# A row maximum carried from chunk to chunk in the score stage of a three-layer attention kernel

## The reference, cut to what matters

```
attn = einsum('bhnd,bhmd->bhnm', qr, kr) + mask          # N = 2304 positions
out  = einsum('bhnm,bhmd->bhnd', softmax(attn, axis=-1), vr)
lepe = conv_general_dilated(v, dw_w, 5x5, feature_group_count=C) + dw_b
```

## Time and profile before

| | |
|---|---|
| median of 3 runs | 3760.14 us (3759.69 to 3761.54) |
| the profiled execution, its own time | 3757.02 us |
| its span from first to last instruction | 3754.9 us |
| mean granted clock of TensorE over the span | 0.963 |
| busy, share of the span | PE 92%, PEld 71%, DVE 74%, ACT 55%, POOL 42% |

### The profile page before, as it was taken

How to read it: one execution, slowest core, us unless ns; L and a number is a source line. 1 busy time by engine, 2 the same in 40 slices (tenths; PEclk the granted TensorE clock), 3 DMA queues, 4 the chain that set the end, 5 groups by cost and what they waited for, 6 DMA issues and landing times. The chain is left out here.

```text
span 3754.9 us, 97899 instructions
## 1 busy us (share of the span) xinstructions
PE 3470.2 (92%) x30782; PEld 2676.2 (71%) x30782; DVE 2794.1 (74%) x6801; ACT 2050.7 (55%) x3661; POOL 1594.4 (42%) x671
## 2 busy tenths in 40 slices
PE   7749999999999999999999999999499999999676
PEld 4437777777777777777777777777287777788555
DVE  6858888888888888888888888886465655544598
ACT  3236666666666666666666666665145454544433
POOL 2336565656656566565656656565100000000223
PEclk8879999999999999999999999999699999999788
DMA  5434224224224223223422422221420201000001
GB/s 172 139 97 125 91 90 129 91 83 111 90 91 128 90 91 105 89 90 100 118 90 97 107 80 97 91 88 46 148 81 14 81 14 40 1 1 0 29 13 38
DMA packets 122409, 307.36 MB, mean 82 GB/s; under 512 B 15609, under 2 KB 85292, under 8 KB 101548
## 3 DMA queue, kind: packets, MB, share of 16 engines
q1 hardware_dynamic: 122284, 305.78, 26.5%
HBM read 251.43 MB, written 54.31 MB: 81 GB/s over the span
## 5 line engine op out<-in xcount | busy, mean ns | idle before, releaser
L729 DVE CUSTOM_DVE_ANT_0 c_S<-c_Sps,mask_tiles 128x768 f32<-128x768 f32 x1728 | 1618.6, 956 | 432.2 <-PE c_Sps L780 391.5
L670 ACT ACTIVATE c_PT<-c_Tps 128x512 f32<-128x512 f32 x2592 | 1428.5, 605 | 872.0 <-PE c_Tps L791 809.4
L642 POOL TENSOR_SCALAR c_S<-c_S,c_row_max 128x2304 f32<-128x2304 f32 x576 | 1411.0, 2450 | 966.4 <-DVE c_row_max L740 966.4
L791 PE MATMUL c_Tps<-ident,c_S 128*128 128x128 f32 x10368 | 1398.6, 273 | 4.1 <-ACT c_PT L670 4.1
L791 PEld LDWEIGHTS c_Tps<-ident,c_S 128*128 128x128 f32 x10368 | 1225.5, 140 | 150.6 <-ACT c_PT L670 9.7
L780 PE MATMUL c_Sps<-c_K,c_Q 96*128 (+1 forms) x3456 | 853.5, 328 | 58.1 <-DMA c_K<-k_parts 41.5
L804 PE MATMUL c_Ops<-c_PT,c_V 128*32 128x256 f32 x10368 | 619.1, 382 | 0.8 <-ACT c_PT L670 0.8
L804 PEld LDWEIGHTS c_Ops<-c_PT,c_V 128*32 128x32 f32 x10368 | 307.4, 109 | 243.7 <-issue 47.7
L780 PEld LDWEIGHTS c_Sps<-c_K,c_Q 96*128 96x128 bf16 x3456 | 314.7, 98 | 219.0 <-issue 144.2
L1245 DVE TENSOR_SCALAR_CACHE_REDUCE l_S<-l_Sps 128x384 f32<-128x384 f32 x432 | 240.3, 557 | 271.0 <-PE l_Sps L1092 242.9
L1022 ACT ACTIVATE l_PT<-l_Tps 128x384 f32<-128x384 f32 x432 | 196.2, 491 | 396.0 <-PE l_Tps L1113 396.0
(11 more groups left out here) (209 smaller groups left out, 1914.7 us busy)
## 6 DMA issues: line engine op xcount, KB each, us to landing
mask_tiles<-in_mask SPq DMA_DIRECT2D x144, 1152.0 KB, 7.8
numerators<-c_O SPq DMA_DIRECT2D x288, 64.0 KB
l_num<-numerators SPq DMA_DIRECT2D x8, 2304.0 KB, 8.4
q_parts<-f_parts SPq DMA_DIRECT2D x12, 576.0 KB, 3.4
k_parts<-f_parts SPq DMA_DIRECT2D x12, 576.0 KB
c_Q<-q_parts SPq DMA_DIRECT2D x72, 96.0 KB
c_K<-k_parts SPq DMA_DIRECT2D x8, 864.0 KB, 8.7
c_vpad<-v_padded SPq DMA_DIRECT2D x8, 756.0 KB, 15.0
```

The costliest lines, as they stand in the source:

```text
L642: pool.tensor_scalar(S[:, slot, :], S[:, slot, :], -1.0, row_max[:, slot:slot + 1], ALU.mult, ALU.add).then_inc(shifted, 1)
L670: act.activation(dst, src, ACT.Exp, scale=-1.0).then_inc(exp_done, 1)
L729: dve.tensor_tensor_reduce(out=S[:, r % ROW_SLOTS, cols(CH, c)].rearrange("p (k n) -> p k n", k=2), in0=Sps[:, n % S_SLOTS, :, 0:GW], in1= ...
L791: last = pe.transpose(Tps[:, g % T_SLOTS, cols(P, k)], S[:, (2 * b + t) % ROW_SLOTS, cols(P, kt)], ident[:, :])
```

## The change

The maximum of a row is no longer put together from three partial maxima. Chunk 0 folds from the constant `LOWEST` as before; chunks 1 and 2 take the maximum that the chunk before them left, read from SBUF as a value per partition, as the initial value of their own fold. Chunk 2's accumulator read then writes `row_max` itself. `row_maximum` and the semaphore `max_ready` go; GpSimd waits for `s_taken` of chunk 2. Since a chunk now reads what the instruction before it wrote, chunks 1 and 2 wait for `s_taken` of the chunk before them, on an empty instruction of its own, ahead of their wait for `s_ready`.

```diff
-        part_max = sb("part_max", [P, 4, NCH])
+        part_max = sb("part_max", [P, 4, NCH - 1])
...
-                            pool.wait_ge(max_ready, ROW_SLOTS * ((2 * hh + hp) * ROUNDS + i) + slot + 1)
+                            pool.wait_ge(s_taken, NCH * (ROW_SLOTS * ((2 * hh + hp) * ROUNDS + i) + slot + 1) + S_SLOTS)
...
             def chunk(ip, p, r, c):
                 n = NCH * r + c
+                slot = r % ROW_SLOTS
+                if c:
+                    dve.wait_ge(s_taken, ROWS * NCH * ip + n + S_SLOTS)
+                    alone(dve)
                 dve.wait_ge(s_ready, ROWS * NCH * ip + n + 1)
                 alone(dve)
+                running = part_max[:, slot, c:c + 1] if c < NCH - 1 else row_max[:, slot:slot + 1]
                 dve.tensor_tensor_reduce(
...
-                    scale=1.0, scalar=LOWEST, op0=ALU.add, op1=ALU.max,
-                    accum_out=part_max[:, r % ROW_SLOTS, c:c + 1]).then_inc(s_taken, 1)
-
-            def row_maximum(ip, r):
-
-                slot = r % ROW_SLOTS
-                dve.wait_ge(s_taken, ROWS * NCH * ip + NCH * (r + 1) + S_SLOTS)
-                dve.tensor_reduce(row_max[:, slot:slot + 1], part_max[:, slot, :], AX.X, ALU.max).then_inc(max_ready, 1)
+                    scale=1.0, scalar=part_max[:, slot, c - 1:c] if c else LOWEST, op0=ALU.add, op1=ALU.max,
+                    accum_out=running).then_inc(s_taken, 1)
...
-                        if c == 0 and r:
-                            row_maximum(ip, r - 1)
-                        if c == 0 and not r and not start:
-                            row_maximum(ip - 1, ROWS - 1)
```

More of the change, by code:

```diff
@@ L512, in layer0_core @@
         s_ready, s_taken = sem("s_ready"), sem("s_taken")
-        max_ready, shifted = sem("max_ready"), sem("shifted")
+        shifted = sem("shifted")
         t_ready, exp_done, pt_used = sem("t_ready"), sem("exp_done"), sem("pt_used")
@@ L762, in _ @@
                     pair(i * 2 + p, p)
-            row_maximum(PAIRS - 1, ROWS - 1)
         @block.tensor
```

## The result

The change makes the kernel slower: 3836.55 us median (3835.42 to 3838.02, 4 runs) against 3759.91 us (3758.69 to 3761.54, 4 runs), a ratio of 1.0204 with a 95% interval of 1.0186 to 1.0221. That is +76.6 us. Forecast were +69 us and 3829 us, in a range of 3776 to 3860 us.

The account below looks back on a forecast made before the run. TensorE sets the pace, tied to VectorE by two PSUM slots. Links and values lose 0.73 + 0.23 = 0.96 us a pair, x 72 = 69 us, on 3757.0 gives 3826, plus 3.1 for the median: 3829 us, range 3776 to 3860.

Parts of the forecast that it names:

- Direction and mechanism: Score stage: slower, chance 0.87; late VectorE makes TensorE lose 0.73 us, mostly at (2,2), and 0.23 us in the second half.
- this sign: TensorE's wait for the accumulator read grows from 0.19 to near 1.15 us a pair; its busy share falls to 96 or 97%.
- The link: Accumulator read's end to start of chunk 1 or 2: 0.29 us, bounds 0.04 to 0.38; eight lie on the sum.
- the prediction's own chain: VectorE from (0,0) to the scores of (2,2), and (4,0) to those of (5,1): 0.96 us a pair lost, 69 us.
- The value: Chunks 1 and 2 reading a [128,1] initial value take 0.05 us longer, bounds 0 and 0.06; nine chunks carry it.
- GpSimd's shift, "nobody waits for it: 0": GpSimd's shift of a row starts about 1 us earlier; no engine waits for it, so its effect is 0.
- the collision with the tap behind (1,2): Rival under longer: shift of row 1 starts together with this tap; all taking 1.74 us adds 24 us, 3850 us.
- The times of the rivals, 3774, 3794, 3850 and 3878 us: Link 0.19; value free; longest taps; link 0.38. Loss of 8 to 45 us: chance 0.22; more than 90: 0.07.
- The reduction, taken as 0: Eight reductions a pair removed, 0.15 us each, 0.08 overlapped: at most 14 us gain, taken as 0.
- The link is short, no change: Rival: link under 0.15 us, VectorE reaches (2,2) as late as before, 3757 to 3760 us; no change has chance 0.09.
- Longer: Rival: link of 0.38 us adds 0.72 us a pair, 52 us, 3878 us; loss above 90 us has chance 0.07.
- Faster: Rival: tap behind (1,2) starts 0.14 us earlier, link under 0.12 us, TensorE waits less: -10 us, 3747 us; chance 0.04.

Follow-up runs that it names:

- e9_short_link_alone: Kernel before, chunks 1 and 2 also wait for the chunk before, without an own empty instruction; reduction, constants and shift time kept: 3757.13 us, -0.3 us (1.0002).
- mended change: Changed kernel with one wait lacking its own empty instruction, GpSimd's shift put back, first tap's padded-input wait moved to the pair's head: 3776.09 us, +19.1 us against kernel before.

## Why the prediction was right, and where it wasn't

*Direction and mechanism: right.* TensorE sets the pace, the reduction's time is worth nothing to it, and the link puts VectorE onto TensorE's path through two slots of PSUM, most of all at (2,2) behind the tap. The wait of TensorE there was to grow from 0.19 us; it is 0.68 us in the pair shown. The size of this sign was off: forecast were 1.15 us a pair and a busy share of 96 or 97%, the list of waits has 0.63 us a pair, and TensorE is busy 97.8%. The rest of its loss is spread so thin that the list doesn't have it: in the median of 40 pairs the scores of (2,2) start 1.62 us behind those of (2,1) in place of 1.12, those of (4,0) 0.16 us later behind (3,2) than before, and nine other chunks 0.03 to 0.11 us later.

*The link: 0.29 us, half right.* Into chunk 1 it is 0.29, as built from the earlier trace rows. Into chunk 2 it is 0.21. The 0.08 that is missing is, by all that the trace shows, the register operation between the two waits: chunk 2 waits for `s_ready` at the same number, 24 ip + n + 1 counted over rows and chunks, at which chunk 1 waited for `s_taken`, so the value is in a register already. The trace has 47 such operations of the `s_ready` wait (L731) in 200 us, one a row and not two. Five of the eight links are of this kind: 5 x 0.08 x 72 = 29 us too much in the sum. Without them the prediction's own chain gives 69 - 29 = 40 us; with the shift put back 44 us were measured (39 to 51). With the measured 0.06 us for the value on nine chunks it is 46 us.

*The value: 0.05 us, measured 0.06* (1016 against 956 ns). Right; without the link it is free (+0.8 us), as was to be expected of a chunk that waits for its scores.

*GpSimd's shift, "nobody waits for it: 0": the step that failed.* That nobody waits for its end holds, as far as the waits show. But it runs 1 us earlier, and at (3,0) and (7,0) it is in VectorE's way: 32 us. The prediction had seen the collision with the tap behind (1,2) and priced it at 24 us as a rival, from the one tap of 1.74 us in the earlier trace rows; there the tap comes first and loses nothing (1.42 us). Which of the two starts first decides, and that could be read from the trace of before, where a shift that starts 0.25 us behind the tap of (3,0) is the long one:

```profile
1571.95 1.41 DVE L722 SCALAR_TENSOR_TENSOR c_conv<-c_vpad,taps,c_conv  x1
```
```profile
1572.20 3.21 POOL L642 TENSOR_SCALAR c_S<-c_S,c_row_max 128x2304 f32<-128x2304 f32 x1 [0.91 <-DVE c_row_max L740]
```


*The total* came out 7.6 us under the measured one because two errors of 29 and 32 us, with opposite signs, met. That part was luck. (The times of the rivals, 3774, 3794, 3850 and 3878 us, leave out the 3.1 us that the sum of 3829 adds for the median.)

*The reduction, taken as 0: right, for its time.* The short link with the value costs 18 us with the reduction kept; the version without it isn't faster (19 us, with the tap's wait moved besides). What it was worth is its place in the instruction stream: the wait added 34 instructions to the loop, the reduction's end took 18 away again, and that kept the loop from being loaded anew. The prediction had no term for this, and in the changed kernel none was needed.

*Rivals.* "The link is short, no change" is shown by e9_short_link_alone for a link of 0.17 to 0.23 us without the value. "Longer" wasn't needed. "Faster" fell as a forecast, but its mechanism, the tap set by the sequencer, was confirmed by moving the wait (-7 us).

*Why the mended change (+19 us) is no better than the version with short link, value and reduction (+18 us), though its tap starts earlier:* the traces show a part of it. With the reduction between (2,0) and (2,1), the link is 0.18 us (first two rows); without it, 0.24 us (last two):

```profile
1577.90 0.08 DVE L734 DVE_READ_ACCUMULATOR2_ANT c_part_max<- 128x1 f32 x1
...
1578.16 1.02 DVE L734 CUSTOM_DVE_ANT_0 c_S<-c_Sps,mask_tiles,c_low 128x768 f32<-128x768 f32 x1
```
```profile
1582.51 0.08 DVE L731 DVE_READ_ACCUMULATOR2_ANT c_part_max<- 128x1 f32 x1
...
1582.83 1.02 DVE L731 CUSTOM_DVE_ANT_0 c_S<-c_Sps,mask_tiles,c_part_max 128x768 f32<-128x768 f32 x1 [0.23 <-DVE c_part_max L731]
```

So in the median of 40 pairs (2,0) starts 0.10 us earlier in the mended change, counted from (0,0), but (2,2) only 0.04 to 0.05 us, and the whole pair is just 0.01 to 0.04 us shorter. What makes the link 0.06 us longer without the reduction stays open.

## What to carry to other kernels

An engine that is busy 83% of the time can still have no slack where two buffer slots tie it to the engine that sets the pace; follow the chain between the two hand-overs with the start of each instruction, and count a new dependence at every place where two instructions overlapped before. When work on an engine that nobody waits for moves in time, ask what it shares with its new neighbour: here an earlier start, a gain on paper, cost 32 us. And in a long unrolled loop count the instructions before adding waits, and look for a gap with the cause "issue" behind its branch.

## What the runs showed of the hardware

- A wait on the instruction just before costs VectorE 0.17 to 0.29 us from the end of its accumulator read to the next start, by how many sequencer instructions stand between; without one the next starts 0.08 us before that end.
- The tap, a VectorE instruction with two inputs in SBUF, and GpSimd's shift in SBUF all but exclude each other: 2.76 in place of 1.41 us for the tap that comes second, 3.2 to 3.4 in place of 2.2 us for the shift that comes second, and the one that came first keeps its time. The chunk, with one input in PSUM, isn't touched (0.95 to 1.02 us).
- A loop of 298 recorded VectorE instructions pays about 3 us at its branch, and 8.6 to 9.0 us in three rounds with the DMA engines over 90% busy; one of 280 pays about 0.3; 34 instructions in idle places, from 264 to 298, cost 128 us in this kernel.
